# Expert results stored to token order by indirect stores per expert pair, in place of gathers at the end

## The reference, cut to what matters

```
x = layernorm(x + attention(x))
scores = sigmoid(x @ gate_w)
selected = top_2(scores + expert_bias)
weight = scores[selected] / sum(scores[selected])
shared = (silu(x @ shared_gate_w) * (x @ shared_up_w)) @ shared_down_w
routed = sum over the two experts e of weight[e] * (silu(g) * u) @ experts_down[e]
         with g, u = split(x @ experts_gate_up[e])
x = layernorm(x + shared + routed)
```

## Time and profile before

| | us |
|---|---|
| median of 3 runs | 979.98 |
| lowest and highest of them | 977.06 and 982.03 |
| span of the profiled execution | 975.7 |
| TensorE busy in the span | 854.0 (88%) |
| VectorE busy | 660.1 (68%) |
| ScalarE busy | 476.2 (49%) |
| GpSimd busy | 300.0 (31%) |

### The profile page before, as it was taken

How to read it: one execution, slowest core, us unless ns; L and a number is a source line. 1 busy time by engine, 2 the same in 40 slices (tenths; PEclk the granted TensorE clock), 3 DMA queues, 4 the chain that set the end, 5 groups by cost and what they waited for, 6 DMA issues and landing times. The chain is left out here.

```text
span 975.7 us, 18404 instructions
## 1 busy us (share of the span) xinstructions
PE 854.0 (88%) x5476; PEld 478.9 (49%) x5477; DVE 660.1 (68%) x1527; ACT 476.2 (49%) x686; POOL 300.0 (31%) x368
## 2 busy tenths in 40 slices
PE   7979799999999989999999997799898999999300
PEld 4635434444444434444444432687556777777200
DVE  6428688888888887888888870489892122466364
ACT  3423266656666656656666566455322444444100
POOL 3423312211112111221112211442477500464373
PEclk9979899999999999999999999889899999999755
DMA  8773855444764266425754000710126745766443
GB/s 285 193 205 131 162 67 75 100 97 59 131 85 89 36 117 118 68 38 106 130 66 57 9 2 25 235 65 23 60 103 210 232 137 152 207 207 211 157 126 95
DMA packets 82464, 113.95 MB, mean 117 GB/s; under 512 B 8945, under 2 KB 60401, under 8 KB 82417
## 3 DMA queue, kind: packets, MB, share of 16 engines
q1 hardware_dynamic: 57808, 78.01, 38.1%
q0 software_dynamic: 6720, 18.88, 5.9%
q10 hardware_dynamic: 17888, 16.41, 5.2%
HBM read 62.55 MB, written 50.33 MB: 116 GB/s over the span
## 5 line engine op out<-in xcount | busy, mean ns | idle before, releaser
L658 ACT ACTIVATE work<-ps 128x1024 f32<-128x1024 f32 (+3 forms) x384 | 293.8, 811 | 185.5 <-PE ps L725 185.3
L335 DVE TENSOR_REDUCE m_neg<-ps 128x1 f32<-128x512 f32 (+3 forms) x432 | 265.6, 662 | 29.2 <-PE ps L320 18.7
L629 POOL TENSOR_SCALAR_AFFINE_SELECT work<-work 128x512 f32<-128x512 f32 x128 | 81.2, 634 | 394.4 <-ACT work L658 390.0
L317 PE MATMUL ps<-stacks 96*128 96x512 bf16 (+3 forms) x528 | 151.9, 332 | 1.5 <-DVE m_neg L335 1.5
L725 PE MATMUL ps<-stacks 99*128 99x512 bf16 (+3 forms) x528 | 124.6, 329 | 6.4 <-PEq L371 4.8
L335 DVE TENSOR_REDUCE m_neg_late<-ps 128x1 f32<-128x384 f32 (+3 forms) x176 | 106.7, 636 | 27.4 <-PE ps L320 27.4
L740 PE MATMUL ps<-work,vg 128*32 128x512 f32 (+3 forms) x1056 | 112.5, 498 | 1.6 <-POOL work L629 1.6
L320 PE MATMUL ps<-mask_b,ident_b 128*128 128x128 bf16 x512 | 100.3, 223 | 0.0
L317 PEld LDWEIGHTS ps<-stacks 96*128 96x128 bf16 x528 | 50.0, 98 | 95.0 <-DVE m_neg L335 48.8
L1243 DVE TENSOR_TENSOR work<-work,ps 128x256 f32<-128x256 f32 x48 | 20.2, 421 | 106.7 <-ACT work L1062 106.7
L1421 PE MATMUL ps<-wgu,work 128*128 x384 | 91.7, 382 | 0.3 <-issue 0.3
(11 more groups left out here) (143 smaller groups left out, 1098.4 us busy)
## 6 DMA issues: line engine op xcount, KB each, us to landing
stacks<-qk_parts SPq DMA_DIRECT2D x132, 128.0 KB, 6.3
qk_parts<-work SPq DMA_DIRECT2D x32, 384.0 KB, 3.0
y_sorted<-work SPq DMA_DIRECT2D x8, 1536.0 KB, 9.9
work<-y_sorted SPq DMA_DIRECT2D x48, 256.0 KB
z_sorted<-work ACTq DMA_DIRECT2D x48, 256.0 KB
wgu<-qk_parts SPq DMA_DIRECT2D x60, 128.0 KB, 6.5
work<-in_xT SPq DMA_DIRECT2D x8, 512.0 KB, 4.8
work<-in_x SPq DMA_DIRECT2D x8, 512.0 KB, 3.6
```

Of the source, the lines that this page charges most:

```text
L317: mm = pe.matmul(dst, qs[r][0:KS, h0 + m, qt * P:(qt + 1) * P], ks[r][0:KS, h0 + m, half * CH:half * CH + w], start=True, stop=not diag)
L335: dve.tensor_reduce(dst, ps[:, bank, 0:heads * w].rearrange("p (h k) -> p h k", h=heads), AX.X, ALU.max, negate=True).then_inc(reduced, 1)
L629: pool.affine_select(out=blk_, in_=blk_, compare_op=ALU.is_ge, fill=0.0, base=0, pattern=[[0, GH], [1, P]], channel_multiplier=-1).then_in ...
L658: act.activation(probs[:, s + 2 * pair:s + 2 * pair + 2, off:CH], ps[:, SCORE_BANK + 2 * pair:SCORE_BANK + 2 * pair + 2, off:CH], ACT.Exp, ...
```

## The change

`z_sorted` and the gathers go. Each row of `y_sorted` becomes 260 words long instead of 256 (`ROW`): behind the 256 values stands the row in `z_back` to which its result belongs. `z_back` holds the results in token order, all first choices and then all second ones, and behind them 512 rows (`TRASH`) that take the results of the filled-up rows. The fill in the attention writes zero rows with such ids, in 24 stores instead of 8.

GpSimd writes the ids of the first choice by one iota, scatters a section's first choices, and, half by half, overwrites the ids by those of the second choice when the half's first scatters have landed. Behind all scatters of both sections it takes the ids of each loaded pair out of `ys` (`take_home`, a copy of two words per partition), and three turns later issues two indirect stores of the pair's result from `zs` into `z_back` (`send_home`). SP's `load_rows` gets one more wait, for the `take_home` that read the slot before. ScalarE stores no results any more.

The gathers at the end become plain loads on SP (`load_z`), one of 256 KB per tile for both choices. VectorE's combines beside the pairs now come four in three turns. Stores of finished chunks move from GpSimd to SP (section 0) and from SP to ScalarE (section 1).

```diff
+ROW = D + 4
+TRASH = TOPK * TILES * P
+TRASHES = 4
+IDS = 6
...
-        z_sorted = [dram(f"z_sorted{g}", (SEC_ROWS, D), F32) for g in range(SECTIONS)]
+        z_back = dram("z_back", (TRASH + TRASHES * P, D), F32)
...
+                            for a in range(part // (P * TRASHES)):
+                                sp.dma_start(y_sorted[q][bass.ds(j * part + a * P * TRASHES, P * TRASHES), :]
+                                             .rearrange("(b p) d -> p b d", p=P), blank)\
+                                    .then_inc(blank_stored, 16)
...
-            LAST_FROM = SEC_PAIRS + 5
+            z_tiles = z_back[0:TRASH, :].rearrange("(j t p) d -> p t j d", j=TOPK, p=P)
+
+            LAST_FROM = SEC_PAIRS + 6
...
+                def load_z(u):
+                    wait_count(sp, both_added, u - ZSLOTS + 1)
+                    sp.dma_start(zg[u % ZSLOTS], z_tiles[:, u]).then_inc(gathered[u % ZSLOTS], 16)
...
+                def beside_rows(n):
+                    if n == LAST_FROM:
+                        z_complete(0)
+                    for u in last_tiles(n):
+                        load_z(u)
+                    c, left = divmod(n - (LAST_FROM + 10), 3)
+                    if 0 <= c < SEC_CHUNKS and left == 0:
+                        store(c)
...
                     def load_rows(n, k2, r):
                         wait_count(sp, ysT_ready, n - 1)
+                        wait_count(sp, home_ready, n - 1)
                         sp.dma_start(ys[r], y_rows[g][:, bass.ds(2 * n - g * SEC_BLOCKS, 2), :])\
                             .then_inc(ys_loaded[r], 16)
...
+                store(SEC_CHUNKS - 1)
+                z_complete(1)
+                for u in range(SEC_TILES, TILES):
+                    load_z(u)
...
+                def scatter(g, j, q):
+                    low = g * SEC_TILES + q * SEC_TILES // 2
+                    high = low + SEC_TILES // 2
+                    if j == 1:
+                        pool.wait_ge(scattered[g][0][q], 16 * SEC_TILES // 2)
+                        write_ids(1, low, high)
+                        pool.wait_ge(ids_written, 2 * g + q + 2)
...
+                def take_home(n):
+
+                    wait_count(pool, z_stored[n % 2], 32 * ((n - IDS) // 2 + 1))
+                    pool.wait_ge(ys_loaded[n % 2], 16 * (n // 2) + 16)
+                    pool.tensor_copy(home[:, n % IDS, :], ys[n % 2][:, :, D].bitcast(U32)).then_inc(home_ready, 1)
+
+                def send_home(n):
+                    pool.wait_ge(home_ready, n + 1)
+                    pool.wait_ge(z_copied, n + 1)
+                    for k in range(2):
                         pool.indirect_dma_start(
-                            out=zg[u % ZSLOTS][:, j, :], out_offset=None, in_=z_sorted[u // SEC_TILES],
-                            in_offset=bass.IndirectOffsetOnAxis(ap=row_of[:, j, u:u + 1], axis=0))\
-                            .then_inc(gathered[u % ZSLOTS], 16)
+                            out=z_back, out_offset=bass.IndirectOffsetOnAxis(ap=home[:, n % IDS, k:k + 1], axis=0),
+                            in_=zs[n % 2][:, k, :], in_offset=None).then_inc(z_stored[n % 2], 16)
...
+                write_ids(0, 0, TILES)
                 staggered(pool, [(0, add_bias), (1, deviation)], CHUNKS)
+                pool.wait_ge(ids_written, 1)
                 for g in range(SECTIONS):
                     pool.wait_ge(rows_ready, g + 1)
...
+                    for j in range(TOPK):
+                        for q in range(2):
+                            scatter(g, j, q)
+                for t in range(PAIRS + 3):
+                    if t < PAIRS:
+                        take_home(t)
+                    c, left = divmod(t - (LAST_FROM + 5), 3)
+                    if 0 <= c < SEC_CHUNKS and left == 0:
+                        second_deviation(c)
+                    if t >= 3:
+                        send_home(t - 3)
+                for c in range(SEC_CHUNKS, CHUNKS):
+                    second_deviation(c)
...
-                        act.dma_start(z_rows[g][:, bass.ds(2 * n - g * SEC_BLOCKS, 2), :], zs[r])\
-                            .then_inc(z_stored[r], 16)
```

More of the change, by code:

```diff
@@ L621, in _ @@
                 pool.memset(vg[2][:, :, :, DK:32], 1.0).then_inc(ones_ready, 1)
-                pool.memset(zero, 0.0).then_inc(zero_ready, 1)
+                pool.memset(blank, 0.0).then_inc(blank_ready, 1)
+                pool.wait_ge(blank_ready, 1)
+                pool.iota(blank[:, :, D:ROW].bitcast(I32), [[P, TRASHES], [0, ROW - D]], base=TRASH,
+                          channel_multiplier=1).then_inc(blank_ready, 1)
                 def mask(i, u):
@@ L891, in build @@
             blocks_ready = sem("blocks_ready")
-            scattered = [sem(f"scattered{g}") for g in range(SECTIONS)]
+            scattered = [[[sem(f"scattered{g}_{j}_{q}") for q in range(2)] for j in range(TOPK)]
+                         for g in range(SECTIONS)]
+            ids_written = sem("ids_written")
+            home_ready = sem("home_ready")
             gate_ready = sem("gate_ready")
@@ L942, in load_rows @@
                         wait_count(sp, ysT_ready, n - 1)
+                        wait_count(sp, home_ready, n - 1)
                         sp.dma_start(ys[r], y_rows[g][:, bass.ds(2 * n - g * SEC_BLOCKS, 2), :])\
                             .then_inc(ys_loaded[r], 16)
[L946 to L950, removed]
+                    for j in range(TOPK):
+                        for q in range(2):
+                            sp.wait_ge(scattered[g][j][q], 16 * SEC_TILES // 2)
+                    staggered(sp, [(0, load_rows)], SEC_PAIRS, base=g * SEC_PAIRS,
+                              until=LAST_FROM if g else None, beside=beside_rows if g else None)
+                store(SEC_CHUNKS - 1)
+                z_complete(1)
+                for u in range(SEC_TILES, TILES):
+                    load_z(u)
                 for c in range(CHUNKS):
@@ L1089, in _ @@
                 act.wait_ge(wgu_loaded, 16)
-                for g in range(SECTIONS):
-                    staggered(act, [(0, turned), (1, silu), (3, result(g))], PAIRS,
-                              turns=(g * (SEC_PAIRS + 3), (g + 1) * SEC_PAIRS + 3))
-                for r in range(2):
-                    act.wait_ge(z_stored[r], 16 * PAIRS // 2)
+                staggered(act, [(0, turned), (1, silu), (3, result)], PAIRS)
+                for c in range(SEC_CHUNKS, CHUNKS):
+                    act.wait_ge(out_ready, c + 1)
+                    act.dma_start(o_v[:, c * CT:(c + 1) * CT, :], acc[c % len(acc)]).then_inc(out_stored[c], 16)
             @blk.vector
@@ L1321, in _ @@
                 staggered(dve, [(0, hidden), (1, hidden_turned)], PAIRS, until=LAST_FROM // 2 * 2, beside=last_stage)
-                for t in range(PAIRS + 1, LAST_FROM + NORM_BEHIND + SEC_TILES):
-                    last_stage(t)
                 for u in range(SEC_TILES, TILES):
```

120 lines of the change are left out of this document (51 added, 69 removed).

## The result

| | before | changed |
|---|---|---|
| median, us | 978.52 (4 runs) | 1009.33 (4 runs) |
| lowest and highest | 976.92 and 982.03 | 1008.07 and 1013.83 |
| span of the profiled execution | 975.7 | 1006.2 |

The changed kernel takes 1.031 of the time before, with an interval from 1.027 to 1.035. The profiled execution took 1008.07 us, with a span of 1006.2. In the span the difference is 30.5 us; 28.2 were predicted. The predicted time, 1008.2, lies nearer to 1009.33 than that: it carried 4.3 us between span and median, and the changed kernel has 3.1.

What follows compares the result with a forecast made beforehand. The prediction took TensorE to bound the expert pairs, with GpSimd's scatters before and a GpSimd and VectorE tail behind. 37.2 + 1.5 + 3.5 - 14.0 = +28.2 us gave span 1003.9, time 1008.2 us; own range 1003 to 1012.

Steps and rivals of the forecast that it cites:

- The stop: Before turn 2, row loads wait for the first ids copy behind all scatters: +37.2 us, bounds 35 to 40.
- The clock: Behind the idle time before turn 2, TensorE runs at a lower granted clock: +1.5 us, bounds 0 to 3.
- The pairs: Expert pairs with GpSimd copying ids and sending results: +3.5 us, an estimate between 0 and 10.
- thin slack in the ring: In the pairs, the loop of result copy, sends, ids copy and row load has only 0.9 us slack.
- a full VectorE: From turn 30 on, VectorE's combines, norms and hidden work fill 10.4 of 10.7 us in three turns.
- rival (a): In the pairs, slower sends or row loads set turns of 3.7 to 3.8 us: +10, 1014.7 us; chance 0.18.
- Wrong if turns were 3.8 us or more: Sign against the forecast in the pairs, where turns of 3.6 to 3.7 us were expected.
- The tail: Behind the last pair, plain z loads replace gathers and VectorE becomes the bound: -14.0 us, bounds -15 to -3.
- The attention: The fill in 24 stores instead of 8 hides in SP's waits: 0 us, bounds -1 and +3.
- (b): Behind the last pair, shared DMA engines or slow loads keep the time as long as before: 1022 us; chance 0.06.
- (d): In the attention, the fill doesn't hide: up to 56 us less slack, so over 1020 us; chance 0.03.
- (c): Before turn 2, GpSimd copies ids early enough, idle time under 10.5 us: faster, 969.5 us without it; chance 0.04.

Runs made afterwards that it cites:

- the ring of 16: Changed kernel with ids copied by VectorE and 16 result slots in `zs` instead of two: 973.52 us, ratio 0.995 to the kernel before.
- the fast version: Changed kernel with ids copied by VectorE, 16 result slots, and section 0's stores issued behind the last row load: 963.41 us, ratio 0.986.
- the last control: The kernel with VectorE ids, 16 result slots and late stores, run again unchanged: 1013.77 us beside 1050.54 for the kernel before, ratio 0.964.

## Why the prediction was right, point by point

**The stop, +37.2 against +35.7.** Right in place, mechanism and size. The last scatter began at 773.53, 0.55 us later than in the earlier trace rows, where 2.0 were allowed; that is nearly all of the 1.5 us by which the term was too large. The four stops cost next to nothing: about 0.18 us each, the iota alone, where I took 0.5. Section 0 itself started 0.8 us later, and this was won back because fewer of the 64 issues were long ones (62.2 us busy against 63.2). GpSimd, in order of time:

```profile
711.85 0.96 POOL L1023 DMA_INDIRECT y_sorted<-v_home,row_of  x1 [0.30 <-issue]
712.82 0.20 POOL L1012 IOTA v_home<- 128x32 int32 x1
713.29 0.99 POOL L1023 DMA_INDIRECT y_sorted<-v_home,row_of  x1 [0.28 <-POOL v_home L1012]
```

**The clock, +1.5 against +1.6.** Right: the granted clock is 0.55 in the stop and 0.70 in the 8 us behind it.

**The pairs, +3.5 against +6.0: the term that was mis-sized,** inside its bounds of 0 to 10 but not for the reasons given. It named thin slack in the ring and a full VectorE. That the sum comes out near is luck: +8.4 and -2.4 us, neither of them foreseen, partly cancel, and the turn of 3.6 to 3.7 us holds only as the average of turns of 3.48 and of 4.32. Two errors lie in it.

The first: the stores of finished chunks in SP's queue had no price at all. The diff's `beside_rows` calls `store(c)`, and I moved the z loads past the row loads but never asked what `store` waits for. It waits for VectorE's norms with a row load behind it, and the row load is slower behind the store; together that costs 8.4 us, and 10 us by the other pairs of profiles (4.496 and 3.618; 4.48 and 3.65). The runs with the stores moved show it by themselves. The rule of my own sum (each wait on a queue: what is queued behind it) was applied to `home_ready` and not to this one.

The second: "ScalarE loses 48 issues of 0.4 us, which weren't in TensorE's way". They probably were in its way. TensorE's waits in the pairs, each from one kernel's own stretch (us in total, times, longest): before from 746 to 900, and changed from 785 to 895:

```profile
PE ps L1411 <- issue: 8.0, 16, 1.1
```

```profile
PE ps L1454 <- DMA work<-y_sorted: 3.7, 11, 0.7
```

In the version with the ring of 16 and late stores the stretch from 780 to 820 shows no such wait, and a turn of 3.25 us:

```profile
780.00:820.00 40.00, 40.00 (x222) 35.01 (x221) 10.71 (x36) 18.27 (x38) 28.99 (x32) 1.00 0.59 180
```

So TensorE's own turn is 3.25 us, and the kernel before took 3.56. With the ids on VectorE it is 3.25 as well in turns 4 to 7, with two result slots, all scatters still running and no DMA on ScalarE. ScalarE in the kernel before, in order of time:

```profile
787.74 0.60 ACT L1069 ACTIVATE work<-ps 128x512 f32<-128x512 f32 x1 [0.70 <-PE ps L1437]
788.52 0.40 ACTq L1072 DMA_DIRECT2D z_sorted<-work  x1
789.10 0.60 ACT L1056 ACTIVATE work<-ps 128x512 f32<-128x512 f32 x1 [0.76 <-ACT work L1069]
```

The store waits for the copy's end and is issued, and only then does ScalarE copy the next turned rows, 0.76 us behind its last work; in the changed kernel it mostly follows directly (799.88 and 807.28, without idle time before them). No run took these stores out of the kernel before and nothing else, so this stays argued. "TensorE-bound at 95%" hid it: 5% idle were 16 waits of up to 1.1 us in some 43 turns, one in each second or third, and there was room of 0.3 us a turn to win. The kernel before had such a turn itself, from 748.26 to 751.51.

The changed kernel has 3.48 us a turn, 0.23 above TensorE's own 3.25, and what it waits for is row loads. So of rival (a) a little is true: the ring's slack of 0.9 us is not quite there, and every third turn takes 3.7 us. With the ids on VectorE this goes. Against the 3.56 of before that is no loss, and so it didn't show. "Wrong if turns were 3.8 us or more" came true for turns 35 to 47 alone, by the stores and not by the ring. The Trainium skill says in "DMA: Bandwidth & Descriptors", under "Issuing engines are not separate DMA queues", that DMAs of all engines share the same 16 DMA engines and interleave. What I made of it, that the row loads grow beside the z loads, is not what made the turns 35 to 47 long: with the z loads in place and only the stores moved they take 3.62 us. It isn't nothing either. In the changed kernel one row load without a store ahead of it, issued at 894.14 behind two z loads, took 4.2 us, and the version with late stores and a ring of 16 takes 3.65 us in those turns against 3.25 before them, with three waits of 0.4 to 0.7 us for row loads. Whether that is the shared traffic or the z loads' place in SP's queue, no run tells apart.

**The tail, -14.0 against -13.7.** Right in mechanism: the first z load is usable 2.8 us after its issue, 16 loads are issued in 22.5 us, and VectorE is the bound at 1.57 us a combine. Two misses of about 1 us cancel: the first combine starts 20.6 us behind turn 47 instead of 19.5, and from there to the last moments it is 29.1 instead of 30.0 us. The end behind it took 0.9 us more.

**The attention, 0.** Right. SP still waits 304.9 us for the maxima (315.8 in the earlier trace rows), and the fill is covered.

**The rivals.** (b) and (d) fell with the tail and the fill. (c), faster, asked for a stop under 10.5 us; that is what the ring of 16 with ids on VectorE brings, by taking the stop away. I had 969.5 us for it, and it took 973.5; without the stores' cost as well, 963.4.

## What to carry to other kernels

Before work is moved into a queue, list for every instruction in it what it waits for and what stands behind it, also for the ones that look like bookkeeping: one copy of two words behind 64 scatters cost 36 us, three stores that wait for norms cost 8 to 10. Work that must only be drained, as results here, can wait in a ring as deep as the longest absence of its engine. And a busy share of 95% is not a bound: compare the average turn with the shortest one that the same trace has (3.56 and 3.25 us here).

## What the runs showed that I had not expected

A tiny copy (0.19 us) or an iota of 32 columns (0.20 us) between two indirect stores costs GpSimd hardly more than itself: the stores on either side of the iota begin 1.44 us apart instead of 1.265 (711.85 and 713.29).

On three chips VectorE and ScalarE stood idle for a time while the scatters ran, with nothing of the core's own that ended it. The clearest rows, from the last control, in order of time ("remote" is the profile's word for such idle time):

```profile
739.24 1.28 ACT L1094 ACT_TABLE_LOAD   x1 [33.19 <-remote]
...
794.21 0.38 ACT L1105 ACTIVATE work<-ps 128x256 f32<-128x256 f32 x1 [16.23 <-remote]
```

The kernel before took 1042 to 1051 us there and 979 elsewhere. Two runs on one of these chips show that it goes with the scatters: without those of section 1 the last such idle time ends at 730.93 (the last scatter begins at 732.7), and with them spread over the pairs it goes on to 848.67 (845.6). The sends, which are indirect stores too but fewer in a turn, mostly have none beside them. Why it comes on some chips and not on others stays open. It also changes verdicts: the fast version took 0.986 of the time before on the one chip and 0.964 on the others, and the changed kernel, 1.031 here, would come out ahead of the kernel before there, at 0.986, if the estimate of 1030 us beside 1044.19 holds.
